# Attention over gathered rows: the rows added on VectorE in PSUM, and one tile in 20 picked on TensorE

## What is computed

```python
xl = (h @ Wl + bl).reshape(n, H, C); xr = (h @ Wr + br).reshape(n, H, C)   # H = 4 heads, C = 32
x_i = xl[dst]; x_j = xr[src]
e = jax.nn.leaky_relu(x_i + x_j, 0.2)
logit = jnp.einsum('ehc,hc->eh', e, att)
m = jax.ops.segment_max(logit, dst, num_segments=n)
ex = jnp.exp(logit - m[dst]); den = jax.ops.segment_sum(ex, dst, num_segments=n)
out = jax.ops.segment_sum((ex / (den[dst] + 1e-16))[..., None] * x_j, dst, num_segments=n) + bias
```

## Time and profile before

| | before |
|---|---|
| median of the runs | 6605.85 us |
| profiled execution, its own time | 6615.38 us |
| its span | 6613.6 us |
| three rounds of attention, first to last gather | 1078 to 2308, 2414 to 3646, 3755 to 4991 us |
| busy: PE, DVE, POOL, ACT | 72%, 60%, 58%, 24% of the span |
| mean granted TensorE clock | 0.84 of full |

### The profile page before, as it was taken

The page is one execution under the profiler, slowest core; times in us unless marked ns, Lnnn a source line. Parts: engine busy times, 40 slices in busy tenths (PEclk is TensorE's granted clock), DMA queues, the critical chain, the costliest instruction groups (busy, mean ns, idle before and its releaser), DMA issues. The chain is left out here.

```text
span 6613.6 us, 138303 instructions
## 1 busy us (share of the span) xinstructions
PE 4770.9 (72%) x35731; PEld 4233.1 (64%) x35732; DVE 3963.6 (60%) x9254; ACT 1607.7 (24%) x3395; POOL 3805.8 (58%) x3122
## 2 busy tenths in 40 slices
PE   7878774888888748888887478888874566666665
PEld 5755334777787647778776478777773455555555
DVE  8987226666666576666665766666666533333334
ACT  4764100111111111111111111111111134444443
POOL 0000003777777737777777277777771078888884
PEclk9999986898999878999998789898886777777777
DMA  6853442333333323333333233333331222222221
GB/s 163 220 161 110 121 119 56 87 93 91 97 97 94 96 68 87 92 96 96 93 94 97 69 82 97 92 94 91 92 99 42 52 69 65 65 66 66 65 65 46
DMA packets 640422, 603.10 MB, mean 91 GB/s; under 512 B 245196, under 2 KB 579098, under 8 KB 639526
## 3 DMA queue, kind: packets, MB, share of 16 engines
q0 software_dynamic: 248480, 231.25, 15.1%
q10 hardware_dynamic: 234095, 211.99, 11.0%
q1 hardware_dynamic: 157719, 158.28, 9.0%
HBM read 498.50 MB, written 99.35 MB: 90 GB/s over the span
## 5 line engine op out<-in xcount | busy, mean ns | idle before, releaser
L563 POOL DMA_INDIRECT rows<-row_table,now x2250 | 2783.6, 1237 | 1780.7 <-issue 1505.8
L563 POOL DMA_INDIRECT rows<-node_table,now x800 | 989.0, 1236 | 563.5 <-issue 563.5
L850 PE MATMUL turn<-xr,ft 125*125 125x132 f32 x7500 | 969.7, 286 | 70.5 <-DVE ft L920 69.2
L850 PEld LDWEIGHTS turn<-xr,ft 125*125 125x125 f32 x7500 | 936.3, 197 | 76.2 <-DVE ft L920 71.1
L951 DVE SCALAR_TENSOR_TENSOR z<-zp,own 125x512 f32<-125x512 f32 x672 | 464.1, 691 | 780.8 <-PE zp L831 775.7
L842 PEld LDWEIGHTS sums<-both,hot 125*125 125x125 f32 x5376 | 765.5, 198 | 179.3 <-issue 117.4
L842 PE MATMUL sums<-both,hot 125*125 125x137 f32 x5376 | 795.5, 293 | 99.1 <-ACT both L737 57.7
L831 PE MATMUL zp<-rows,ident 125*125 x2700 | 809.9, 426 | 37.7 <-SPq L588 37.7
L828 PE MATMUL zp<-parts,hot_t 125*125 x8100 | 649.9, 232 | 240.2 <-issue 190.1
L828 PEld LDWEIGHTS zp<-parts,hot_t 125*125 125x125 bf16 x8100 | 607.9, 144 | 275.0 <-issue 273.2
L736 ACT CAST hot<-hot 125x500 f32<-125x500 bf16 x672 | 408.7, 608 | 1510.8 <-PE sums L842 898.8
(11 more groups left out here) (454 smaller groups left out, 5572.7 us busy)
## 6 DMA issues: line engine op xcount, KB each, us to landing
hot<-hots ACTq DMA_DIRECT2D x896, 122.1 KB
hot_t<-hots_t ACTq DMA_DIRECT2D x678, 122.1 KB
counts<-pairs SPq DMA_DIRECT2D x55, 685.1 KB
rows<-row_table,now POOLq DMA_INDIRECT x2250, 3.6
spread_slots<-slot_table POOLq DMA_DIRECT2D x56, 488.3 KB, 5.4
hots_t<-hot_t SPq DMA_DIRECT2D x112, 218.8 KB
hots<-hot_dst SPq DMA_DIRECT2D x112, 218.8 KB
pairs<-cells SPq DMA_DIRECT2D x25, 685.1 KB
```

Of the source, the lines that this page charges most:

```text
L563: pool.indirect_dma_start(rows[:, q, j, :], None, table, bass.IndirectOffsetOnAxis(ap=now[:, n, lane + j:lane + j + 1], axis=0)).then_inc( ...
L850: ins = pe.matmul(mixture, hot_n[:, w, :], xr[:, w, :], start=w == 0, stop=w == WIN - 1)
```

## The change

`PICK` becomes 5: the last tile of each fifth quad is picked, 40 tiles a round instead of 50. Four are made ahead of the steps (`FIRST`), then one in each of three groups (`PER`) of blocks 0 to 11; the fourth group of these blocks picks none. The two identity matmuls and PE's wait for `here` are gone from `spread_rows`. DVE waits for `here` itself and adds the gathered rows to `zp` in place, waits for that instruction (`joined`), and goes on as before. For that it reads the places of four steps as well.

```diff
-PICK = 4
+PICK = 5
+PER = 3
+FIRST = 4
-LAST = (PICKS - 2) // GROUP
+LAST = (PICKS - FIRST) // PER
...
             def spread_rows(k, m, q, source):
...
                     for part in range(3):
-                        pe.matmul(zp[:, p, j, 0:ROW], hot_t[:, q, j * P:(j + 1) * P], own[part], start=part == 0 and j % 2 == 0, stop=False, skip_group_check=True)
-                hold(pe, here, (quad & 255) + 1, held_up_too)
-                for half in range(2):
-                    ins = pe.matmul(zp[:, p, 2 * half:2 * half + 2, 0:ROW], g.ident[0:P, 0:P], rows[:, bass.ds(at, 1), 2 * half:2 * half + 2, :].rearrange("p a j f -> p (a j) f"),
-                                    start=False, stop=True, skip_group_check=True)
+                        ins = pe.matmul(zp[:, p, j, 0:ROW], hot_t[:, q, j * P:(j + 1) * P], own[part], start=part == 0 and j % 2 == 0, stop=part == 2, skip_group_check=True)
                 ins.then_inc(spread, 1)
...
-            for t in range(2):
+            for t in range(FIRST):
                 for r in range(len(CUTS)):
                     pick(t, r)
             pe.wait_ge(own_ready, 1)
...
-            def logits(k, i, q):
+            def logits(k, i, q, place):
                 p, s = q % 2, bass.ds(HALF * AHEAD * i + HALF * q, HALF)
+                quad, at, _ = place
+                dve.wait_ge(here, (quad & 255) + 1)
                 dve.wait_ge(spread, after(k))
+                both_sides = zp[:, p, :, 0:ROW]
+                dve.tensor_tensor(both_sides, both_sides, rows[:, bass.ds(at, 1), :, :].rearrange("p a j f -> p (a j) f"), ALU.add).then_inc(joined, 1)
+                dve.wait_ge(joined, after(k))
                 dve.wait_ge(reduced, after(k, 2))
...
                     if picking:
                         choose(b, i, q)
-                    for stage, _ in enumerate(logits(k, i, q)):
+                    if q == 0:
+                        places = step_places(nc, dve, g, k)
+                        pairs = step_pairs(nc, dve, g, c)
+                    for stage, _ in enumerate(logits(k, i, q, places[q])):
                         if stage == 0:
-                            if q == 0:
-                                pairs = step_pairs(nc, dve, g, c)
                             weigh(c, i, q, pairs[q][0])
...
+            def block_of(b, per):
+                both(b, 0, per > 0)
+                if per > 1:
+                    with dve.Fori(1, per) as i:
+                        both(b, i, True)
+                if per < GROUP:
+                    with dve.Fori(max(per, 1), GROUP) as i:
+                        both(b, i, False)
```

More of the change, by code:

```diff
@@ L772, in _, with spreads @@
             act.wait_ge(laid, 2)
-            load_srcs(GROUP + 2)
-            with act.Fori(0, GROUP) as i:
+            load_srcs(PER + FIRST)
+            def spreads(i):
                 for q in range(AHEAD):
                     load_spread(AHEAD * i + q + 2, (q + 2) % AHEAD)
-                store_picked(i + 2)
+            with act.Fori(0, PER) as i:
+                spreads(i)
+                store_picked(i + FIRST)
+            if PER < GROUP:
+                with act.Fori(PER, GROUP) as i:
+                    spreads(i)
             for q in range(2):
@@ L780, in _, with group @@
             weigh(0)
[L782 to L790, removed]
+            def group(b, i):
+                for q in range(AHEAD):
+                    k, c = BSTEPS * b + AHEAD * i + q, BSTEPS * b + AHEAD * i + q - BSTEPS
+                    widen(c, GROUP * b + i - GROUP, i, q)
+                    load_spread(k + 2, (q + 2) % AHEAD)
+                    load_hot(c + 2, (q + 2) % AHEAD)
+            def block_of(b, per):
+                if per:
+                    with act.Fori(0, per) as i:
+                        group(b, i)
+                        store_picked(PER * b + i + FIRST)
+                if per < GROUP:
+                    with act.Fori(per, GROUP) as i:
+                        group(b, i)
                 weigh(b)
@@ L878, in four_steps @@
                     k = BSTEPS * b + AHEAD * i + q
-                    if q or not isinstance(i, int):
+                    if q or not (isinstance(i, int) and i == 0):
                         sum_rows(k - BSTEPS - 1, (q - 1) % AHEAD)
@@ L883, in four_steps @@
                     if picking and q:
-                        pick(GROUP * b + i + 2, q - 1)
+                        pick(PER * b + i + FIRST, q - 1)
                     spread_rows(k + 1, GROUP * b + i + (q + 1) // AHEAD, (q + 1) % AHEAD, places[q])
-            for t in range(2):
+            for t in range(FIRST):
                 for r in range(len(CUTS)):
@@ L914, in _ @@
         def _(dve):
-            begin(dve, scaled, reduced, summed, weighted, accd)
+            begin(dve, scaled, reduced, summed, weighted, accd, joined)
             def point(t, i, r):
@@ L1029, in _, with alone @@
             dve.wait_ge(laid, 2)
-            with dve.Fori(0, GROUP) as i:
+            def alone(i, picking):
                 for q in range(AHEAD):
-                    choose(0, i, q)
-                    for _ in logits(AHEAD * i + q, i, q):
-                        pass
+                    if picking:
+                        choose(0, i, q)
+                    if q == 0:
+                        places = step_places(nc, dve, g, AHEAD * i)
+                    for _ in logits(AHEAD * i + q, i, q, places[q]):
+                        pass
+            with dve.Fori(0, PER) as i:
+                alone(i, True)
+            if PER < GROUP:
+                with dve.Fori(PER, GROUP) as i:
+                    alone(i, False)
             softmax(0)
             def both(b, i, picking):
-                first = isinstance(i, int)
+                first = isinstance(i, int) and i == 0
                 for q in range(AHEAD):
```

67 lines of the change are left out of this document (39 added, 28 removed).

## The result

| | before | after |
|---|---|---|
| median of the runs | 6605.58 us (6600 to 6618, 8 runs) | 6584.84 us (6577 to 6592, 8 runs) |
| ratio | | 0.9964, 95% interval 0.9953 to 0.9975 |
| profiled execution: span, granted clock | 6613.6 us, 0.84 | 6583.6 us, 0.79 |
| gathers of rounds one, two, three | 1229.9, 1232.5, 1235.4 us | 1246.3, 1208.3, 1207.9 us |
| block, median of blocks 1 to 11 of each round | 88.2, 87.9, 88.7 us | 88.9, 85.3, 85.4 us |

The kernel is 21 us faster; 100 were forecast. Rounds two and three lose 24 and 28 us each, and round one becomes 16 us slower. In all that follows a line number of the changed kernel is that of its own file: L976 is the addition, L979 the relu, L844 the spread, L854 the sums, L862 the picks, L577 SyncE's release of the ring.

What follows compares the result with a forecast made beforehand. PE bound the stepping blocks; after the change POOL's gathers would, by a hair: 1196.5 us a round against 1229.9, -33.4, three rounds -100, so 6615.4 becomes 6515, and 6506 us for the median; range 6465 to 6600.

Steps and rivals of the forecast that it cites:

- The addition, 0.74 us from start to start: DVE's new addition in each step: 0.71 us long, plus 0.03 us for waiting on its result; bounds 0.60 and 1.20.
- POOL's floor of 83.4 us a block: POOL's gathers in a steady block: 54.3 of them at 1.536 us each make 83.4 us.
- the first stop: POOL's wait at the first filling of the ring: from 15.4 to 24.1 us, with 12.6 for two more early picks.
- The parts given for block 0: DVE's block 0: 16 steps of 0.74 + 0.72 + 0.72 + 0.4, 9 comparisons of 1.2, some 3 us of loads: 55.4 us.
- The block: ... 82.4 us: DVE's block: three groups of 17.2 us, one of 15.4, 17.5 for softmax and edges, less the end wait for PE.
- PE stops being the bound if its clock holds: PE's work in a picking group falls from 16.3 to some 12.5 us, plus 1.4 us of load: 13.9 us.
- the rival on the clock: PE falls to its lower clock, 0.71, and stays the pace: block 88 us, 6606 us in all; chance 0.09.
- 17.2: A picking group on DVE: 13.4 us of work, four additions of 0.74, 0.6 for loads, 0.2 for register instructions: 17.2 us.
- 1196.5: POOL's gathers of a round: 760 x 1.536 + 24.1 + 5 = 1196.5 us against 1229.9.
- a reserve: DVE's margin behind POOL: 26 us over 13 periods, 2 us a block or 0.12 us a step.
- the gain of 100 us: Whole kernel: 33.4 us less in each round, three rounds -100 us.
- DVE paces the blocks: Rival: DVE sets the blocks' pace, less than PE did; 3 us more a block, 6546 us; chance 0.23.

Runs made afterwards that it cites:

- picks_only_b: The changed kernel with the addition given back to PE, one tile in 20 picked: 6523.8 us, 0.9861 of the kernel before; 0.9817 where that takes 7045 us.
- pick_few_c: The changed kernel with 19 of 25 windows left out of PE's picks, so picked rows are incomplete: 0.9840 of the kernel before (6612 us).
- add_only_b: The kernel before with only the addition moved to DVE, one tile in 16 picked as before: 1.0024 of the kernel before, +13.4 us.
- acc_first: The changed kernel with DVE's accumulation of two steps earlier put ahead of the addition: 0.9696 of the kernel before (7045 us).
- half_add_b: The changed kernel with the rows of two of a step's four tiles left out of DVE's addition: 0.9885 of the kernel before (6612 us).
- group 1: A set of follow-up kernels run on one chip beside the kernel before, which took 7045 us there; transfers were waited for longer.
- after_again: The changed kernel itself, unaltered, run again where the kernel before took 6617 us: 6588.1 us, ratio 0.9955.
- after_third: The changed kernel itself, unaltered, run again on a chip where loads land late: 7125.1 us, 0.9733 of the kernel before.

## Why the prediction was wrong

- *The addition, 0.74 us from start to start*: right. 0.715 us long, the relu 0.75 behind it where nothing is issued between, 0.83 otherwise.
- *POOL's floor of 83.4 us a block, and the first stop*: right. picks_only_b and pick_few_c sit at 82.8 to 83.9; the first addition came at 1143.86, 12.9 us later against 12.6 forecast, and the first stop was 21.2 us against 24.1. (The parts given for block 0 add up to 55.1 us and not 55.4.)
- *"The block: ... 82.4 us"*: this is the term that failed; 88.9, 85.3 and 85.4 us were measured in the three rounds. The first part of the miss, 38 us in round one alone, is code loading, which was no term at all: the diff and the order showed the third copy of the step code, and I read its instructions but not its length. That the stall is the place of the code is shown by the moves, which send it to another round or away; its price is shown by the rounds of the changed kernel itself.
- *"PE stops being the bound if its clock holds"*: the second part. The clock fell to 0.80 to 0.91 in picking groups of round two, as the rival on the clock has it, and PE's work in them was 14.1 to 15.9 us where 12.5 were forecast. The fall comes with the move of the addition: add_only_b has it, picks_only_b doesn't. PE stood still before these slow matmuls, for its own loads and for DVE's accumulation; which of the waits brings the clock down isn't shown, and in acc_first, without the second, it stayed down. Nor does any run hold the clock up with the addition on DVE, so the clock's share of the miss stays open. Groups cost 17.3, 18.0 and 18.6 us against 17.2, the block 85.3; rounds two and three took 1208 us of gathers against 1196.5. That is 11.6 us in each round, 35 in all; 38 + 35 = 73 us, where the two profiled executions are 30 us apart and 70 are missing; 5 us more lie between the rounds, and rounds two and three of before were 8 us longer than round one, which I had used for all. That the block hangs on both engines is shown by pick_few_c and half_add_b: I had added up DVE's chain and PE's chain apart, each with a reserve, but they hang on each other.
- *The whole*: the gain of 100 us was there, with 93 in picks_only_b; I put it down to both halves together, on the premise that PE at 16.3 us a group had to lose its identity matmuls. It had to lose only the pick of one group: picks_only_b keeps groups of 17.3 to 17.8 us, and its block is 83.
- Of the rivals, "DVE paces the blocks" named 3 us a block more and 6546 us; with the 38 us of fetches on top that is the result within 1 us. The 3 us are near what DVE's blocks had in rounds two and three, but the fetches are a mechanism that the rival did not have, so that the sum agrees is in part luck.

The version to keep of those that ran is picks_only where the kernel before takes 6610 us. In group 1 (7045 us) the changed kernel with its code moved has the lower ratio, 0.9655 and 0.9676 against 0.9817. What makes loads land late there, and so which kernel is better in general, stays open.

## What to carry to other kernels

Change one thing where two can be told apart: the halves here are worth -93 and +13 us, and together -29. When work moves from one engine to another and both stand in one loop, add up the loop through both, not each engine's list; and when a loop body grows by a copy, count its instructions and look at the packets of the instruction queue per round. A wait of some 3 us "for issue" at a loop's first instruction, in one copy of a code and not in another, is that.

## What the runs showed of the hardware

- Code of a loop of 306 instructions is fetched again in each turn or not, by where it lies: five packets of 8.2 KB and, in the changed kernel, 3.6 us a turn (block 88.9 against 85.3). In no run here was a loop of 252 instructions (picks_only) or fewer.
- The same program can take 6588 or 7125 us (after_again, after_third): in round two POOL waits 47 us for SP in the one and 249 in the other, and in 2700 to 3500 us DVE's addition waits 106.0 us for something that the profile calls remote, where it waits 10.0 for SP's count of the rows in the one. The packets of the gathers are there as early in both (the last one 3.3 and 3.1 us behind the issue, medians), so what is late isn't seen in them. The kernels differ in how they bear it, so a ratio of half a per cent says nothing beyond the place where it was taken.
- A vector instruction that adds in place in PSUM costs as much as one that writes to SBUF: 0.715 us for 528 elements against 0.692 for 512.
